# Banded attention with a feed-forward branch: score blocks in pairs on four PSUM banks shared with the attention outputs

## Chip, cores and metric

The kernel runs on one core of one Trainium2 chip, in one launch. The metric is the device time of that launch in microseconds (us); less is better. All inputs and outputs are float32.

## What is computed

x is 8 batches of 1024 rows of 512 numbers. Each row is normalised (mean, variance), and on the result stand an attention branch and a feed-forward branch, both added to x:

```python
def _L0_attn_ref(x, Wq, bq, Wk, bk, Wv, bv, Wo, bo):       # 16 heads of 64, N = 1024, E = 512
    Q = (x @ Wq + bq).reshape(B, N, 16, 64).transpose(0, 2, 1, 3)      # K and V in the same way
    scores = jnp.einsum('bhid,bhjd->bhij', Q, K)
    band = jnp.abs(idx[None, :] - idx[:, None]) <= 64
    columns = jnp.where(band, scores, 0.0)                 # outside the band the score is 0, not -inf
    attn = jax.nn.softmax(columns, axis=-1)
    out = (attn @ V).transpose(0, 2, 1, 3).reshape(B, N, 1024)
    return out @ Wo + bo

def _L0_ffn_ref(x, Win, bin_, W1, b1, W2, b2, Wout, bout):  # M = 64, INNER = 16
    s = x @ Win + bin_
    h = relu(s[..., None] * W1 + b1)
    g = einsum('btmh,mh->btm', h, W2) + b2
    return g @ Wout + bout

xn = layernorm(x)
return x + _L0_attn_ref(xn, ...) + _L0_ffn_ref(xn, ...)
```

## The kernel before

Five instruction streams (TensorE `pe`, VectorE `dve`, ScalarE `act`, GpSimd `pool`, SyncE `sp`) are written out by hand and meet at counting semaphores. There is no scheduler: the order in the code is the order on each engine. Each number that is multiplied is split into a high part and a low part of float32r, and each product is three passes (`PASSES`: high by high, high by low, low by high).

**Steps.** The work is a pipeline of 66 steps, one for each of 8 batches x 8 pairs of heads, and two to run out. Step n projects values, queries and keys of unit n (a pair of heads; `project`, line 811), attends for unit j = n - 1 (scores, softmax, weighting of the values), and projects out for unit o = n - 2 (`project_out`, line 822, eight tiles of 128 rows). `run_steps` writes out the steps: pairs 2 to 5 of a batch are an inner hardware loop (`middle`), batches 1 to 7 an outer one. Pairs 0 and 1 of a batch also carry the feed-forward branch (`ffn_first`, `ffn_last`), pair 6 the statistics of the next batch, pair 7 its normalisation (`ln_next`), pair 0 the last transposes of it (`ln`). 64 steps attend.

**Scores.** `scores(tp)`, for tp = 0 to 3, is two tiles of 128 queries, each against 256 keys, for both heads of the pair: 3 passes x 2 heads x 2 tiles = 12 matmuls. A head has 64 rows, so the two heads' matmuls stand in the two halves of the array and are recorded as a pair (x2). The results go to the two banks `score[0]` and `score[1]`, one for each head. VectorE's `mask_scores(tp)` (line 594) multiplies them by the band mask into `probs`, takes the row maxima and counts `masked`, four for each block. `scores(tp)` waits until the block before it is masked, since there is one pair of banks.

**Softmax and outputs.** ScalarE's `exps(tp)` (line 382) takes the exponentials, VectorE's `denominators(half)` (line 604) the reciprocals, GpSimd's `normalise_weights(half)` (line 301) scales. TensorE transposes the weights (`transpose_weights(u)`, line 867, into `pT_ps`) and weighs the values (`weigh_values(u)`, line 884) for u = 0 to 3, where u % 2 is the head and u // 2 the half of the queries; the result goes to bank `o_ps[h]`. ScalarE copies one half of it (`output_half(u)`, line 427), VectorE adds (`output_sum(u)`, line 647), counting `o_summed`, four for each step. `weigh_values(u)` waits for `o_summed` 4j + u - 1.

**The order around the change.** TensorE in a step: scores(0), V half 0, out(0), scores(1), out(1), V half 1, scores(2), out(2), Q half 0, scores(3), out(3), transposes of u = 0, out(4), and so on, to weigh_values(2), weigh_values(3), eight transposes of the values (line 856). V half 0 goes to bank `fill[0]` and waits for `v_lo` of the step before (line 653). out(0) goes to `fill[1]`, out(1) to `fill[0]`, which ScalarE's `value_lines(0)` (line 398) must have read (`v_in`). V half 1 goes to `fill[1]` and waits for the addition of out(0) on VectorE (`add_output`, line 615, `out_added`). out(4) waits for `qk_lo`, which VectorE counts when it has made `qT_lo` (`qk_low`, line 630) behind ScalarE's `qk_high` (line 412).

VectorE in a step: mask(0), out(0)'s addition, mask(1), out(1)'s addition, denominators(0), mask(2), out(2)'s addition, `qk_low(0)`, out(3)'s addition, mask(3), `weights_low(0)`; at the end out(7)'s addition, `qk_low(3)`, output_sum(2), values_low(0), output_sum(3), values_low(1). ScalarE at the end: output_half(2), values_high(0), output_half(3), values_high(1); values_high(0) waits for the transposes of the values.

The eight PSUM banks before are `fill` (2), `score` (2), `pT_ps` (2), `o_ps` (2).

Of the kernel before, what the change touches and what calls it, by code (L numbers as in the profile page):

```python
# [22 lines left out]
ACT = mybir.ActivationFunctionType  # L23
# [15 lines left out]
def band_attention_ffn(nc, x, Wq, bq, Wk, bk, Wv, bv, Wo, bo, Win, bin_, W1, b1, W2, b2, Wout, bout, out):  # L39
# [14 lines left out]
    with ExitStack() as ctx:  # L54
# [56 lines left out]
        fill = [bank("fill0"), bank("fill1")]  # L111
        score = [bank("score0"), bank("score1")]
        pT_ps = [bank("pT_ps0"), bank("pT_ps1")]
        o_ps = [bank("o_ps0"), bank("o_ps1")]
        ffn_banks = pT_ps + fill
# [228 lines left out]
        def _(act):  # L344
# [18 lines left out]
            for i in range(3):  # L363
# [3 lines left out]
            act.wait_ge(bias_T, 1)  # L367
            act.activation(bias_qkv[:].rearrange("p i h o -> p (i h o)"), score[0][:, 0:3 * PAIRS], ACT.Copy) \
                .then_inc(bias_in, 1)
# [3 lines left out]
            def step(n, b, pair, proj=True, attend=True, ln=False, ln_next=False, ffn_first=False, ffn_last=False,  # L373
# [49 lines left out]
                def output_half(u):  # L423

                    h = u % 2
                    act.wait_ge(pv_done, 4 * j + u + 1)
                    act.activation(o_part[h][h * D:h * D + D], o_ps[h][D - h * D:2 * D - h * D], ACT.Copy) \
                        .then_inc(o_half, 1)
# [118 lines left out]
        def _(dve):  # L547
# [33 lines left out]
            def step(n, b, pair, proj=True, attend=True, out_proj=True, ln=False, ln_next=False, stats_next=False,  # L581
# [4 lines left out]
                def mask_scores(tp):  # L586
                    due = in_register(dve, 4 * j + tp + 1)
                    dve.wait_ge(scored, 1)
                    dve.wait_ge(scored, due)
                    for h in range(2):  # L590
                        for i in range(2):
                            c, t = column(tp, h, i), 2 * tp + i

                            dve.tensor_tensor_reduce(out=probs[:, h, t], in0=score[h][:, i * WIN:i * WIN + WIN],  # L594
                                                     in1=mask[:], scale=1.0, scalar=0.0, op0=ALU.mult, op1=ALU.max,
                                                     accum_out=row_max[:, c:c + 1]).then_inc(masked, 1)
                    dve.wait_ge(masked, 16 * j + 4 * tp + 4)
                    cols = slice(4 * tp, 4 * tp + 4)
                    dve.tensor_scalar(neg_max[:, cols], row_max[:, cols], -1.0, None, ALU.mult).then_inc(max_ready, 1)  # L599
# [40 lines left out]
                def output_sum(u):  # L640
                    h, half = u % 2, u // 2
                    rows = slice(h * D, h * D + D)
                    dve.wait_ge(o_half, 4 * j + u + 1)
                    dve.wait_ge(v_back_ready, j + 1)
                    if h == 0 and begun(2 * j - 1 + half):
                        dve.wait_ge(oT_lo, 2 * j - 1 + half)
                    dve.scalar_tensor_tensor(o_sum[half][rows], o_ps[h][rows], v_back[rows], o_part[h][rows],
                                             ALU.add, ALU.add).then_inc(o_summed, 1)
# [134 lines left out]
        def _(pe):  # L783
# [3 lines left out]
            pe.wait_ge(const_in, 16 * N_CONST)  # L787
            pe.transpose(score[0][:, 0:3 * PAIRS], bias_rows[:], ident[0:3 * PAIRS, 0:3 * PAIRS]).then_inc(bias_T, 1)

            def step(n, b, pair, proj=True, attend=True, out_proj=True, ln=False, ln_next=False,  # L790
                     ffn_first=False, ffn_last=False, after_ffn=False, **_):
                j, o = n - 1, n - 2
                def scores(tp):
                    if tp == 0:
                        pe.wait_ge(qk_lo, 4 * j + 4)
                    if begun(16 * j + 4 * tp):
                        pe.wait_ge(masked, 16 * j + 4 * tp)
                    for i in range(2):
                        t = 2 * tp + i
                        for a, (qp, kp) in enumerate(PASSES):  # L800
                            for h in range(2):
                                rows = slice(h * D, h * D + D)
                                last = pe.matmul(score[h][:, i * WIN:i * WIN + WIN], qT[qp][rows, t * P:t * P + P],  # L803
                                                 kT[kp][rows, t * P:t * P + WIN], start=(a == 0), stop=(a == 2))
# [67 lines left out]
                def weigh_values(u):  # L872
                    half, h = u // 2, u % 2
                    pe.wait_ge(pT_lo, 8 * j + 2 * u + 2)
                    if u == 0:
                        pe.wait_ge(v_lo, 2 * j + 2)
                    if begun(4 * j + u - 1):
                        pe.wait_ge(o_summed, 4 * j + u - 1)
                    for k in range(5):
# [3 lines left out]
                        for part in (hi, lo):  # L883
                            last = pe.matmul(o_ps[h][:, q0:q0 + (end - first) * P],  # L884
                                             v[:, (4 * half + k) % T, h].rearrange("p a d -> p (a d)"),
# [8 lines left out]
                if attend:  # L894
                    scores(0)
                if ln:
                    transpose_x(b, 4)
                    transpose_x(b, 5)
# [15 lines left out]
                if ln:  # L914
                    transpose_x(b, 6)
                    transpose_x(b, 7)
                if attend:
                    scores(1)
                if out_proj and not proj:
# [12 lines left out]
                if attend:  # L932
                    scores(2)
                if out_proj and not proj:
                    project_out_last(2)
# [3 lines left out]
                if proj:  # L939
                    pe.wait_ge(v_in, 2 * n + 2)  # L940
                    project(Q_, 0, qk_proj, fill[QK_BANK[0]])
                if attend:
                    scores(3)
                if out_proj and not proj:
# [118 lines left out]
```

## Time and profile before

| | us |
|---|---|
| median of 3 runs | 2547.38 |
| lowest, highest | 2533.61, 2549.32 |
| span of the profiled execution | 2553.6 |
| TensorE busy in it | 2428.0 (95%) |
| VectorE busy | 1987.7 (78%) |
| ScalarE busy | 1701.5 (67%) |
| GpSimd busy | 1208.9 (47%) |

The rows in the section further down are all of the profiled execution. A row of the timeline has its start in us, its length in us, the engine, the line of the code, the operation, output <- inputs and a count; in brackets stands how long the engine was idle before it, and for whom it waited. Matmuls overlap: what counts is the distance from one start to the next. A row of the waits has who waited for whom, the total in us, how many times, and the longest. A row of the windows has the stretch, its length, then each engine's busy us with its count of instructions (TensorE's matmuls, its weight loads, VectorE, ScalarE, GpSimd), the clock that TensorE was granted (1.00 is all of it), the share of the DMA engines and GB/s.

### The profile page before, as it was taken

Reading aid. Unit: us, or ns where it says so; the run is one execution under the profiler, and the core shown is the slowest. Engines: PE = TensorE matmul, PEld = TensorE weight load, DVE = VectorE, ACT = ScalarE, POOL = GpSimd, SP = SyncE. Lnnn points to the kernel's source line nnn. Section 1 sums busy time; section 2 is a strip of 40 time slices with the busy share of each in tenths; the row PEclk is TensorE's granted clock in tenths of the full one; section 3 lists DMA queues with packets and bytes.
Section 4 is the critical chain, followed back from the end, with each engine's and each line's share of the span. In section 5 each row is a group of like instructions: output and inputs, shape, how many; then the busy total and the mean of one; then the engine's idle time right before and its main releaser. Section 6 shows DMA issues by size and latency. Waiting matters only on the chain.

```text
span 2553.6 us, 50140 instructions
## 1 busy us (share of the span) xinstructions
PE 2428.0 (95%) x14913; PEld 2006.8 (79%) x14913; DVE 1987.7 (78%) x5025; ACT 1701.5 (67%) x4458; POOL 1208.9 (47%) x1515
## 2 busy tenths in 40 slices
PE   4999999999999999999999999999999999999997
PEld 3788787888778787787877878778887788878886
DVE  3777888778887788777887777877779778797777
ACT  3666776667766677666775667756677666766665
POOL 2444445445454454544454444544546444464443
PEclk9999999999999999999999999999999999999999
DMA  3010112110121110201103011031010210012101
GB/s 118 22 30 20 34 30 87 33 34 18 34 83 33 34 29 23 92 24 34 34 17 100 21 30 34 17 100 33 18 34 19 98 33 30 22 52 65 33 21 38
DMA packets 130239, 106.04 MB, mean 42 GB/s; under 512 B 5736, under 2 KB 104064, under 8 KB 130048
## 3 DMA queue, kind: packets, MB, share of 16 engines
q1 hardware_dynamic: 130048, 103.72, 13.3%
q8 instruction: 92, 1.51, 0.3%
q14 instruction: 99, 0.81, 0.1%
HBM read 86.93 MB, written 16.78 MB: 41 GB/s over the span
## 4 chain that ended last, share of the span: by engine, by line
PE 71%; DVE 7%; issue 6%; ACT 6%; DMA 4%; POOL 3%; SPq 1%; DVEq 0%; ACTq 0%; POOLq 0%
PE fill L811 33%; PE fill L822 12%; PE o_ps L884 9%; PE pT_ps L867 7%; PE score L803 5%; ACT probs L382 3%; DMA w_raw<-in_L_attn_Wv 2%; DVE probs L594 2%; DMA out_x<-acc 2%; POOL acc L314 1%; POOL probs L301 1%; PE fill L856 1%; PE fill L849 1%; PE pT_ps L841 1%; ACT v L439 1%
## 5 line engine op out<-in xcount | busy, mean ns | idle before, releaser
L301 POOL TENSOR_SCALAR probs<-probs,inv_l,neg_e 128x256 f32<-128x256 f32 x1024 | 598.7, 598 | 778.6 <-DVE neg_e L609 778.6
L811 PE MATMUL fill<-xT_hi,w_hi 128*128 128x512 f32 x1536 | 627.0, 408 | 26.3 <-ACT vT L404 6.7
L382 ACT ACTIVATE probs<-probs,neg_max 128x256 f32<-128x256 f32 x1024 | 510.8, 501 | 154.1 <-DVE neg_max L599 152.4
L811 PE MATMUL fill<-xT_lo,w_hi 128*128 128x512 f32 x1536 | 608.5, 396 | 0.0
L811 PE MATMUL fill<-xT_hi,w_lo 128*128 128x512 f32 x1536 | 605.9, 394 | 0.0
L615 DVE TENSOR_TENSOR acc<-fill,acc 128x512 f32 (+1 forms) x512 | 350.6, 685 | 100.8 <-PE fill L822 93.6
L594 DVE CUSTOM_DVE_ANT_0 probs<-score,mask 128x256 f32<-128x256 f32 x1024 | 372.5, 421 | 33.6 <-issue 20.6
L811 PEld LDWEIGHTS fill<-xT_hi,w_hi 128*128 128x128 f32 x1536 | 293.7, 191 | 108.7 <-issue 26.6
L420 ACT ACTIVATE pT_hi<-pT_ps 128x512 fp32r<-128x512 f32 x512 | 278.2, 592 | 137.4 <-PE pT_ps L867 137.4
L307 POOL TENSOR_TENSOR oT_lo<-o_sum,oT_hi 128x512 fp32r<-128x512 f32 x128 | 171.1, 1337 | 411.3 <-ACT oT_hi L434 411.3
L811 PEld LDWEIGHTS fill<-xT_hi,w_lo 128*128 128x128 f32 x1536 | 292.5, 190 | 65.4
L811 PEld LDWEIGHTS fill<-xT_lo,w_hi 128*128 128x128 f32 x1536 | 293.6, 191 | 56.1
L637 DVE TENSOR_TENSOR pT_lo<-pT_ps,pT_hi 128x512 fp32r<-128x512 f32 x512 | 327.9, 682 | 1.4 <-ACT pT_hi L420 1.3
L884 PE MATMUL o_ps<-pT_hi,v 128*128 128x256 f32 (+1 forms) x1280 | 307.8, 279 | 0.0
L884 PE MATMUL o_ps<-pT_lo,v 128*128 128x256 f32 (+1 forms) x1280 | 305.5, 279 | 0.0
L867 PEld LDWEIGHTS pT_ps<-ident,probs 128*128 128x128 f32 x2048 | 242.8, 142 | 47.2 <-DVE pT_lo L637 9.8
L867 PE MATMUL pT_ps<-ident,probs 128*128 128x128 f32 x2048 | 273.5, 277 | 6.3 <-DVE pT_lo L637 4.8
L280 POOL TENSOR_TENSOR w_lo<-w_raw,w_hi 128x512 fp32r<-128x512 f32 x192 | 248.0, 1292 | 52.6 <-ACT w_hi L349 52.6
L822 PE MATMUL fill<-wo_hi,oT_hi 128*128 128x512 f32 x512 | 233.9, 457 | 32.1 <-DVE acc L615 21.6
L884 PEld LDWEIGHTS o_ps<-pT_lo,v 128*128 128x128 f32 x1280 | 243.2, 190 | 2.6
L884 PEld LDWEIGHTS o_ps<-pT_hi,v 128*128 128x128 f32 x1280 | 242.5, 189 | 2.6
L630 DVE SCALAR_TENSOR_TENSOR qT_lo<-fill,bias_qkv,qT_hi 128x512 fp32r<-128x512 f32 x128 | 95.8, 748 | 147.2 <-ACT qT_hi L412 147.2
(104 smaller groups left out, 4252.2 us busy)
## 6 DMA issues: line engine op xcount, KB each, us to landing
w_raw<-in_L_attn_Wv SPq DMA_DIRECT2D x64, 256.0 KB, 3.3
w_raw<-in_L_attn_Wq SPq DMA_DIRECT2D x64, 256.0 KB, 3.7
w_raw<-in_L_attn_Wk SPq DMA_DIRECT2D x64, 256.0 KB, 2.7
acc<-in_L_attn_x SPq DMA_DIRECT2D x8, 2048.0 KB, 9.3
wo_raw<-in_L_attn_Wo SPq DMA_DIRECT2D x64, 256.0 KB, 2.8
out_x<-acc SPq DMA_DIRECT2D x7, 2048.0 KB, 7.7
acc<-in_L_attn_x SPq DMA_DIRECT2D x2, 1024.0 KB, 6.7
out_x<-acc SPq DMA_DIRECT2D x2, 1024.0 KB, 4.3
```

Source lines behind the costliest of these rows:

```text
L280: pool.tensor_tensor(w[lo][:, i], w_raw[:, i], f32(w[hi][:, i]), ALU.subtract).then_inc(w_lo, 1)
L301: pool.tensor_scalar(probs[:, h, t], probs[:, h, t], inv_l[:, c:c + 1], neg_e[:, c:c + 1], ALU.mult, ALU.add).then_inc(normed, 1)
L307: pool.tensor_tensor(oT[lo][:, cols], o_sum[half][:], f32(oT[hi][:, cols]), ALU.subtract) \
L382: act.activation(probs[:, h, t], probs[:, h, t], ACT.Exp, bias=neg_max[:, c:c + 1], accum_out=row_sum[:, c:c + 1])
L420: act.activation(pT[u % 2][hi][:, k * LINE:k * LINE + LINE], pT_ps[k][:], ACT.Copy) \
L594: dve.tensor_tensor_reduce(out=probs[:, h, t], in0=score[h][:, i * WIN:i * WIN + WIN], in1=mask[:], scale=1.0, scalar=0.0, op0=ALU.mult, o ...
L615: dve.tensor_tensor(acc[:, parity, t], bank[:], acc[:, parity, t], ALU.add).then_inc(out_added, 1)
L637: dve.tensor_tensor(pT[u % 2][lo][:, cols], pT_ps[k][:], f32(pT[u % 2][hi][:, cols]), ALU.subtract).then_inc(pT_lo, 1)
L811: last = pe.matmul(dst[:], w[wp][:, i, k], xT[xp][:, k, half * LINE:half * LINE + LINE], start=(k == 0 and a == 0), stop=(k == KC - 1 and ...
L822: last = pe.matmul(dst[:], oT[op][:, t * P:t * P + P], wo[wp][:], start=(a == 0), stop=(a == 2))
L867: last = pe.transpose(pT_ps[k][:, i % 4 * P:i % 4 * P + P], probs[:, h, t, c * P:c * P + P], ident[:])
L884: last = pe.matmul(o_ps[h][:, q0:q0 + (end - first) * P], v[:, (4 * half + k) % T, h].rearrange("p a d -> p (a d)"), pT[h][part][:, first ...
```

## The change

The four banks of scores and outputs become one pool `attn[0..3]`. Block tp of the scores goes to `attn[2 * (tp % 2) + h]`, so blocks 0 and 2 have banks 0 and 1, blocks 1 and 3 banks 2 and 3. The output of u goes to `attn[u]`. On TensorE, scores(1) moves up to stand directly behind scores(0), and scores(3) directly behind scores(2). The waits follow the banks: scores(0) waits for the first two output sums of the step before, scores(1) for all four of them (`o_summed` 4j), scores(2) and scores(3) for the masks of two blocks before; `weigh_values(0)` and `weigh_values(2)` wait for the masks of blocks 2 and 3, and no longer for `o_summed`. The order of VectorE, ScalarE and GpSimd is as before, and no instruction is added or left out.

```diff
-        score = [bank("score0"), bank("score1")]
+        attn = [bank(f"attn{i}") for i in range(4)]
+        score = [[attn[2 * i + h] for h in range(2)] for i in range(2)]
+        o_ps = attn
         pT_ps = [bank("pT_ps0"), bank("pT_ps1")]
-        o_ps = [bank("o_ps0"), bank("o_ps1")]
...
                 def scores(tp):
                     if tp == 0:
                         pe.wait_ge(qk_lo, 4 * j + 4)
-                    if begun(16 * j + 4 * tp):
-                        pe.wait_ge(masked, 16 * j + 4 * tp)
+                    if tp >= 2:
+                        pe.wait_ge(masked, 16 * j + 4 * tp - 4)
+                    elif begun(4 * j + 2 * tp - 2):
+                        pe.wait_ge(o_summed, 4 * j + 2 * tp - 2)
...
-                                last = pe.matmul(score[h][:, i * WIN:i * WIN + WIN], qT[qp][rows, t * P:t * P + P],
+                                last = pe.matmul(score[tp % 2][h][:, i * WIN:i * WIN + WIN], qT[qp][rows, t * P:t * P + P],
...
                 def weigh_values(u):
-                    if begun(4 * j + u - 1):
-                        pe.wait_ge(o_summed, 4 * j + u - 1)
+                    if h == 0:
+                        pe.wait_ge(masked, 16 * j + 4 * half + 12)
...
-                            last = pe.matmul(o_ps[h][:, q0:q0 + (end - first) * P],
+                            last = pe.matmul(o_ps[u][:, q0:q0 + (end - first) * P],
...
                 if attend:
                     scores(0)
+                    scores(1)
                 if ln:
                     transpose_x(b, 4)
                     transpose_x(b, 5)
...
-                if attend:
-                    scores(1)
...
                 if attend:
                     scores(2)
+                    scores(3)
...
-                if attend:
-                    scores(3)
```

`output_half`, `output_sum` and `mask_scores` name the new banks (`o_ps[u]`, `score[tp % 2][h]`) and are otherwise the same.

On TensorE, in the inner loop, between out(0) and out(1) (the row of line 822 at the top is the last matmul of out(0), the one at the bottom the first of out(1); `score` is the block scores(1)), before:

```order
L822 MATMUL fill<-wo_hi,oT_lo 128x512
L797 REGISTER_ALU
L803 MATMUL score<-kT_hi,qT_hi 128x256 [waits masked]
L803 MATMUL score<-kT_hi,qT_hi 128x256
L803 MATMUL score<-kT_lo,qT_hi 128x256 x2
L803 MATMUL score<-kT_hi,qT_lo 128x256 x2
L803 MATMUL score<-kT_hi,qT_hi 128x256 x2
L803 MATMUL score<-kT_lo,qT_hi 128x256 x2
L803 MATMUL score<-kT_hi,qT_lo 128x256 x2
L922 REGISTER_ALU
L822 MATMUL fill<-wo_hi,oT_hi 128x512 [waits v_in]
```

The same place in the changed kernel, where line 825 is `project_out`:

```order
L825 MATMUL fill<-wo_hi,oT_hi 128x512 [waits oT_lo]
L825 MATMUL fill<-wo_lo,oT_hi 128x512
L825 MATMUL fill<-wo_hi,oT_lo 128x512
L924 REGISTER_ALU
L825 MATMUL fill<-wo_hi,oT_hi 128x512 [waits v_in]
```

Block 1 is gone from between them: out(1) with its wait for `v_in` stands directly behind out(0).

On TensorE, in the inner loop, at the start of a step of the changed kernel (`attn` is scores here; the first row is the last pair of scores(0), line 811 the wait ahead of V half 0 and line 814 its first matmul):

```order
L806 MATMUL attn<-kT_hi,qT_lo 128x256 x2
L806 MATMUL attn<-kT_hi,qT_hi 128x256 [waits o_summed]
L806 MATMUL attn<-kT_hi,qT_hi 128x256
L806 MATMUL attn<-kT_lo,qT_hi 128x256 x2
L806 MATMUL attn<-kT_hi,qT_lo 128x256 x2
L806 MATMUL attn<-kT_hi,qT_hi 128x256 x2
L806 MATMUL attn<-kT_lo,qT_hi 128x256 x2
L806 MATMUL attn<-kT_hi,qT_lo 128x256 x2
L907 ISA
L811 ISA [waits ffn_added,v_lo]
L814 MATMUL fill<-xT_hi,w_hi 128x512 [waits w_lo]
```

Before, the same place was this:

```order
L803 MATMUL score<-kT_hi,qT_lo 128x256 x2
L903 ISA
L808 ISA [waits ffn_added,v_lo]
L811 MATMUL fill<-xT_hi,w_hi 128x512 [waits w_lo]
```

Block 1 with its wait for `o_summed` now stands between scores(0) and V half 0.

## Rows read from the trace of the kernel before

**Rows 1.** The page: span, and busy us, share and instructions of each engine.
```profile
span 2553.6 us, 50140 instructions
PE 2428.0 (95%) x14913; PEld 2006.8 (79%) x14913; DVE 1987.7 (78%) x5025; ACT 1701.5 (67%) x4458; POOL 1208.9 (47%) x1515
```

**Rows 2.** The waits of TensorE: us in total, times, longest us.
```profile
PE score L803 <- issue: 15.3, 6, 2.7
PE fill L822 <- DVE qT_lo L630: 9.4, 7, 1.8
PE fill L811 <- ACT vT L404: 6.7, 9, 1.8
PE fill L811 <- DVE v L653: 5.1, 21, 0.2
PE score L803 <- DVE row_max L594: 4.6, 4, 2.0
```

**Rows 3.** The timeline of TensorE, step n = 3, from scores(0) to V half 1.
```profile
149.96 0.28 PE L803 MATMUL score<-kT_hi,qT_lo 64*128 64x256 f32 x2
150.38 0.49 PE L811 MATMUL fill<-xT_hi,w_hi 128*128 128x512 f32 x1
...
153.00 0.39 PE L811 MATMUL fill<-xT_hi,w_lo 128*128 128x512 f32 x1
...
153.68 0.39 PE L822 MATMUL fill<-wo_hi,oT_lo 128*128 128x512 f32 x1
154.00 0.39 PE L803 MATMUL score<-kT_hi,qT_hi 64*128 64x256 f32 x2
154.22 0.28 PE L803 MATMUL score<-kT_lo,qT_hi 64*128 64x256 f32 x2
...
154.69 0.28 PE L803 MATMUL score<-kT_hi,qT_lo 64*128 64x256 f32 x2
154.90 0.50 PE L822 MATMUL fill<-wo_hi,oT_hi 128*128 128x512 f32 x1
155.24 0.40 PE L822 MATMUL fill<-wo_lo,oT_hi 128*128 128x512 f32 x1
...
155.72 0.40 PE L811 MATMUL fill<-xT_hi,w_hi 128*128 128x512 f32 x1
```

**Rows 4.** The timeline of VectorE in the same step.
```profile
149.56 0.69 DVE L653 TENSOR_TENSOR v<-fill,v 128x512 fp32r<-128x512 f32 x1 [0.88 <-ACT v L439]
150.28 0.76 DVE L647 SCALAR_TENSOR_TENSOR o_sum<-o_ps,v_back,o_part 64x512 f32<-64x512 f32 x1
...
155.12 0.42 DVE L594 CUSTOM_DVE_ANT_0 probs<-score,mask 128x256 f32<-128x256 f32 x1
...
164.46 0.75 DVE L630 SCALAR_TENSOR_TENSOR qT_lo<-fill,bias_qkv,qT_hi 128x512 fp32r<-128x512 f32 x1 [2.38 <-ACT qT_hi L412]
165.12 0.68 DVE L615 TENSOR_TENSOR acc<-fill,acc 128x512 f32<-128x512 f32 x1
165.72 0.42 DVE L594 CUSTOM_DVE_ANT_0 probs<-score,mask 128x256 f32<-128x256 f32 x1
```

**Rows 5.** The timeline of ScalarE: the eviction of V half 0.
```profile
153.43 0.60 ACT L398 ACTIVATE vT<-fill 128x512 f32<-128x512 f32 x1 [1.11 <-PE fill L811]
153.92 0.19 ACT L398 ACTIVATION_READ_ACCUMULATOR vT<-fill 128x1 f32 x1
```

**Rows 6.** The timeline of TensorE: the first matmul of out(4).
```profile
165.63 0.48 PE L822 MATMUL fill<-wo_hi,oT_hi 128*128 128x512 f32 x1
```

**Rows 7.** Windows: step n = 3, and step n = 9, the second of a batch.
```profile
149.26:184.91 35.65, 35.50 (x225) 29.68 (x224) 27.45 (x73) 23.83 (x67) 16.74 (x22) 1.00 0.10 29
376.77:420.81 44.04, 42.44 (x251) 33.76 (x250) 40.95 (x90) 33.05 (x77) 28.69 (x29) 1.00 0.19 63
```

**Rows 8.** The timeline of TensorE, step n = 50: a matmul behind a wait of 1.78.
```profile
2001.08 0.49 PE L822 MATMUL fill<-wo_hi,oT_hi 128*128 128x512 f32 x1 [1.78 <-DVE qT_lo L630]
```

**Rows 9.** Windows: after that wait, and after one of 2.0 in the last step.
```profile
2003.00:2008.00 5.00, 5.00 (x32) 4.42 (x31) 4.50 (x11) 4.82 (x14) 1.84 (x4) 1.00 0.00 0
2516.00:2520.00 4.00, 3.77 (x27) 2.83 (x27) 2.99 (x12) 3.30 (x14) 0.00 (x0) 0.64 0.00 0
```

More of the change, by code:

```diff
@@ L367, in _ @@
             act.wait_ge(bias_T, 1)
-            act.activation(bias_qkv[:].rearrange("p i h o -> p (i h o)"), score[0][:, 0:3 * PAIRS], ACT.Copy) \
+            act.activation(bias_qkv[:].rearrange("p i h o -> p (i h o)"), attn[0][:, 0:3 * PAIRS], ACT.Copy) \
                 .then_inc(bias_in, 1)
@@ L426, in output_half @@
                     act.wait_ge(pv_done, 4 * j + u + 1)
-                    act.activation(o_part[h][h * D:h * D + D], o_ps[h][D - h * D:2 * D - h * D], ACT.Copy) \
+                    act.activation(o_part[h][h * D:h * D + D], o_ps[u][D - h * D:2 * D - h * D], ACT.Copy) \
                         .then_inc(o_half, 1)
@@ L592, in mask_scores @@
                             c, t = column(tp, h, i), 2 * tp + i
-                            dve.tensor_tensor_reduce(out=probs[:, h, t], in0=score[h][:, i * WIN:i * WIN + WIN],
+                            dve.tensor_tensor_reduce(out=probs[:, h, t], in0=score[tp % 2][h][:, i * WIN:i * WIN + WIN],
                                                      in1=mask[:], scale=1.0, scalar=0.0, op0=ALU.mult, op1=ALU.max,
@@ L646, in output_sum @@
                         dve.wait_ge(oT_lo, 2 * j - 1 + half)
-                    dve.scalar_tensor_tensor(o_sum[half][rows], o_ps[h][rows], v_back[rows], o_part[h][rows],
+                    dve.scalar_tensor_tensor(o_sum[half][rows], o_ps[u][rows], v_back[rows], o_part[h][rows],
                                              ALU.add, ALU.add).then_inc(o_summed, 1)
@@ L787, in _ @@
             pe.wait_ge(const_in, 16 * N_CONST)
-            pe.transpose(score[0][:, 0:3 * PAIRS], bias_rows[:], ident[0:3 * PAIRS, 0:3 * PAIRS]).then_inc(bias_T, 1)
+            pe.transpose(attn[0][:, 0:3 * PAIRS], bias_rows[:], ident[0:3 * PAIRS, 0:3 * PAIRS]).then_inc(bias_T, 1)
             def step(n, b, pair, proj=True, attend=True, out_proj=True, ln=False, ln_next=False,
```

## The prediction, made before the changed kernel was run

> **What bounds the kernel now.** I read the page first: its span and the busy shares [rows 1]. TensorE is busy for 95% of 2553.6 us, VectorE for 78%, so anything that makes TensorE wait or lets it run closer together moves the end one for one, unless another engine was about to be waited for. Next come TensorE's waits [rows 2]: apart from the lead-in and the eight steps around a batch's first pairs they are small, and no row there names an attention output or `o_summed`. Last, one ordinary step (the fourth, n=3) in order of time, on TensorE [rows 3], VectorE [rows 4] and ScalarE [rows 5]. What the reader is to see there: TensorE pays for each visit to the scores, and VectorE and ScalarE work through a chain that runs behind it with little room.
>
> I call the first value projection of a step V0, the second V1, the first query projection Q0, and the output projections out(0) to out(7).
>
> **The gain.** A score block is 12 matmuls on 64 rows, in pairs, between matmuls on all 128 rows. In [rows 3], around scores(1): the last full matmul starts at 153.68, the first score pair at 154.00, 0.32 later where full matmuls follow each other in 0.24 (155.24 to 155.72 is two of them): 0.08. The second pair comes 0.22 after the first, where pairs otherwise follow in 0.12 (154.22 to 154.69 is four of them): 0.10. Going out, 154.69 to 154.90 is 0.21 instead of 0.12: 0.09, and 154.90 to 155.24 is 0.34 instead of 0.24: 0.10. Together 0.37; with 0.23 as the pace, which V0 shows (153.00 to 153.68 is three matmuls), it is 0.39, and I take that. The change removes two such visits in each of 64 steps: 128 x 0.39 = 50 us. [...]
>
> **The new wait.** Score block 1 now writes banks 2 and 3 of the shared four, which the last two attention outputs of the previous step used. It waits for `o_summed` 4j, so for the previous step's last `output_sum`, and stands directly behind scores(0). In [rows 4] that addition runs from 150.28 to 151.04. A release of TensorE by VectorE takes 0.13: `v` ends at 150.25 and V0, which waits for it, starts at 150.38 [rows 3, 4]. So scores(1) starts at 151.17. It could have started at 149.96 + 0.12 = 150.08: a wait of 1.09 us. Queued behind it on TensorE is everything. Its six pairs take 0.22 + 4 x 0.12, then 0.21 to leave: V0 starts at 152.08 instead of 150.38, 1.70 later (of this, 0.70 is work that came earlier than before, and the 0.2 that V0 waited in any case is used up).
>
> Does it hit every step? Not the first step (nothing before it), not the eight that follow the feed-forward output (24 matmuls stand between), not the six that follow the end of the inner loop, where TensorE already sat up to 2.7 us with no named releaser [rows 2]. 64 - 1 - 8 - 6 = 49 steps have it.
>
> **What stood behind scores(1).** scores(1) used to lie between out(0) and out(1), and was cover. out(1) needs the eviction of V0's bank by ScalarE: that starts 0.43 after V0's last matmul (153.00 to 153.43) and its accumulator read ends 0.68 later [rows 5]; with 0.13 for the release, out(1) may start 1.24 after V0's last matmul. TensorE would be there after 4 x 0.23 = 0.92. So out(1) loses 0.32 and starts 153.00 + 1.70 + 1.24 = 155.94, which is 1.04 later than 154.90. V1 follows at 156.76; the first output addition, begun 0.43 after out(0)'s last matmul (155.38), takes 0.69 [rows 4] and is released at 156.63, so it does not stop V1. After V1 the second merge gives back its 0.39: +0.65 from there.
>
> **What is late next.** VectorE keeps its order, so mask(1) stands behind that addition: 155.81 + 0.60 (the pace from 165.12 to 165.72) = 156.41 where it was 155.12. The chain mask(1), exponentials, denominators, mask(2), exponentials, `qT_hi`, `qT_lo` passes back and forth between VectorE and ScalarE and moves as a whole by 1.29. `qT_lo` ends at 164.46 + 0.75 + 1.29 = 166.50 [rows 4], and Q0's own later end puts it some 0.07 further; TensorE is released at 166.7. out(4), which waits for it, would have started at 165.63 [rows 6] + 0.65 = 166.28. It loses 0.4. The step is then 1.05 us longer. VectorE catches up at the step's end, where it waits for out(7), so the next step starts from the same picture.
>
> **The sum.** In later batches V0 waited some 0.1 longer already (21 small waits, [rows 2]), so I take 1.0 for the 26 ordinary steps: 26 us. The eight steps that normalise the next batch have ScalarE later still: Q0 already waits for ScalarE there, one of the nine of [rows 2], so the whole 1.29 comes through: 8 x 1.3 = 10. In the seven steps with n = 9, 17, ... VectorE is busy for 40.95 of 44.04 us [rows 7], no room for a lag: 7 x 1.3 = 9. In the seven first steps of a batch (n = 8, 16, ...) the transposes of the new x also stand behind scores(1), and their evictions stand ahead of mask(0) on VectorE; I carry 1.8 of the 1.9 that TensorE is late: 7 x 1.8 = 13. The six behind the loop end: first merge free, but mask(0) and its additions were late there already, 0.15 each: 1. The eight after the feed-forward output: scores(1) is free, out(1) loses its cover, and in seven of them out(4) waits for `qT_lo` anyway, up to 1.8 [rows 2]: 0. First and last step: -1. Sum: 26 + 10 + 9 + 13 + 1 + 0 - 1 = +58. The profiled execution would go from 2553.6 to 2611.6. Its own time lies 6 above the median of the three runs, 2547.4, so I predict 2605 us.
>
> The other edits cost nothing: the outputs' wait for `masked` instead of `o_summed` is met microseconds before by mask(2) and mask(3), which the same engine's later work depends on; scores(2) and scores(3) wait for masks that are two blocks old. If that cover went, it would be at most one mask block, four times 0.42 us [rows 4].
>
> Bounds of the terms: the 1.09 wait is read to 0.05. What the lag adds is the soft part. If none of it reaches TensorE, the direct terms stand alone: 49 waits leave 0.65 each, less 0.1, and 15 free steps give back up to 0.78: 27 - 12 = +15. If the whole 1.9 of V0's delay and more contention came through in the 22 special steps and 1.29 in the ordinary ones, it is 26 x 1.3 + 22 x 1.9 = +76.
>
> **The rivals.**
> *Only direct terms* (+15, 2562 us; down to 0): ScalarE's exponentials catch up in their gaps. For it: VectorE sat idle 2.38 us before `qT_lo` [rows 4]. Against it: that gap is named as waiting for ScalarE, so it belongs to the chain.
> *The merge wins*, the other side of zero. Place: scores(1) at the step's start. Price: the `o_summed` wait. If that wait were below about 0.45 us instead of 1.09, out(1) and the chain would barely move and the 0.78 a step would win; with no wait at all, 2547 - 50 = 2497 us, with half the gain 2520. For it: the toll is plainly in [rows 3]. Against it: the last `output_sum` ends at 151.04 by its own chain, behind two evictions on ScalarE, which the change does not touch.
> [...]
>
> **How the numbers follow.** My forecast 0.72 (its own range 2580 to 2625), direct terms only 0.14, the merge wins 0.06, the clock 0.08. Range: 2562 to 2630 holds the forecast and most of the direct case, and leaves out the clock and the merge's win. A measurement of this kernel can tell about 1% from no change, that is 25 us. Faster by over 1%: 0.05. Within 1%: 0.15, the direct case and a part of the merge's. Slower by over 1%: 0.80.
>
> **What would show it.** TensorE's waits should hold a new row, `attn` scores behind `o_sum`, 49 times, mean 0.9 to 1.1, some 50 us in all; a row of out(1) behind `vT` (0.3 each); and out(4) behind `qT_lo` far above its 7 of now. The score blocks should come in pairs without the 0.22 and 0.34 in the middle. An ordinary step should take 36.7 instead of 35.65 [rows 7]. Wrong it would be if the last `output_sum` came earlier than 1.8 us after scores(0) begins, or if `qT_lo` were ready when out(4) comes.

## The result and the profile after

| | before | after |
|---|---|---|
| median of 4 runs | 2541.7 us | 2602.9 us |
| lowest, highest | 2533.6, 2549.3 | 2594.1, 2617.3 |
| span of the profiled execution | 2553.6 | 2592.4 |

The change makes the kernel slower: 1.025 times the time, interval 1.020 to 1.030. Run again (e11, below) it was 1.023, 1.021 to 1.026. The forecast was 2605 us and slower. It stood on a median of 2547.4 before; a fourth run brings that to 2541.7.

The page of the changed kernel, with its span, its engines and the chain of work that ended last, answers to [rows 1]:

```profile
span 2592.4 us, 49953 instructions
PE 2409.6 (93%) x14913; PEld 1997.7 (77%) x14913; DVE 1978.6 (76%) x5025; ACT 1693.5 (65%) x4458; POOL 1210.8 (47%) x1515
...
PE 54%; DVE 16%; ACT 15%; issue 11%; DMA 2%; POOL 1%; SPq 1%; DVEq 1%; ACTq 0%; POOLq 0%
```

TensorE is busy 18 us less, and the span is longer: it waits. The 18 us do not measure the gain of the merges: a step as below has 35.40 where it had 35.50 [rows 7], and with the guard of e6 on both sides the difference is 4 us (2414.9 in e6, 2410.5 in e9). The waits of TensorE and of its weight loads, changed kernel (engine, line, for whom: us in total, times, longest), where [rows 2] had nothing of the first, 7 of the second and nothing of the third:

```profile
PE attn L806 <- DVE o_sum L648: 56.4, 55, 2.7
PE fill L825 <- DVE qT_lo L631: 36.7, 53, 2.3
...
PEld fill L825 <- ACT vT L399: 28.6, 55, 0.5
```

The ordinary step n = 3 of the changed kernel, TensorE in order of time; line 806 is the scores, 814 the projections, 825 the output projection. It answers to [rows 3] and [rows 6]:

```profile
150.32 0.28 PE L806 MATMUL attn<-kT_hi,qT_lo 64*128 64x256 f32 x2
151.45 0.38 PE L806 MATMUL attn<-kT_hi,qT_hi 64*128 64x256 f32 x2 [0.86 <-DVE o_sum L648]
...
152.35 0.50 PE L814 MATMUL fill<-xT_hi,w_hi 128*128 128x512 f32 x1
...
155.02 0.39 PE L814 MATMUL fill<-xT_hi,w_lo 128*128 128x512 f32 x1
...
156.19 0.50 PE L825 MATMUL fill<-wo_hi,oT_hi 128*128 128x512 f32 x1
...
167.07 0.49 PE L825 MATMUL fill<-wo_hi,oT_hi 128*128 128x512 f32 x1 [0.37 <-DVE qT_lo L631]
```

The step begins at 149.62. scores(1) waits until the last output sum is there. V0 starts 2.73 us into the step where it was 1.12 (150.38 - 149.26), out(1) at 6.57 instead of 5.64, and out(4) at 17.45 instead of 16.37, behind `qT_lo`. VectorE and ScalarE in the same step, answering to [rows 4, 5]:

```profile
150.64 0.76 DVE L648 SCALAR_TENSOR_TENSOR o_sum<-attn,v_back,o_part 64x512 f32<-64x512 f32 x1
...
156.13 0.69 DVE L616 TENSOR_TENSOR acc<-fill,acc 128x512 f32<-128x512 f32 x1 [1.33 <-PE fill L825]
156.74 0.41 DVE L595 CUSTOM_DVE_ANT_0 probs<-attn,mask 128x256 f32<-128x256 f32 x1
...
166.19 0.75 DVE L631 SCALAR_TENSOR_TENSOR qT_lo<-fill,bias_qkv,qT_hi 128x512 fp32r<-128x512 f32 x1 [2.54 <-ACT qT_hi L413]
```

```profile
155.45 0.60 ACT L399 ACTIVATE vT<-fill 128x512 f32<-128x512 f32 x1 [2.78 <-PE fill L814]
155.94 0.19 ACT L399 ACTIVATION_READ_ACCUMULATOR vT<-fill 128x1 f32 x1
...
165.34 0.69 ACT L413 ACTIVATE qT_hi<-fill,bias_qkv 128x512 fp32r<-128x512 f32 x1
```

The last output sum ends 1.78 us into the step, as before (151.04 - 149.26). mask(1) starts at 7.12 instead of 5.86: VectorE now waits 1.33 for out(0).

Windows of the changed kernel (stretch, length, busy us of TensorE, its weight loads, VectorE, ScalarE, GpSimd, clock, DMA share, GB/s): step 3, then 16 and 17 (the first two of a batch), then 10 and 18 (the third of a batch), which answer to [rows 7]:

```profile
149.62:186.35 36.73, 35.40 (x225) 29.66 (x224) 27.32 (x73) 23.74 (x67) 16.69 (x22) 1.00 0.10 29
654.31:699.27 44.96, 41.73 (x257) 34.42 (x257) 35.86 (x82) 31.98 (x78) 23.18 (x26) 1.00 0.07 21
699.27:744.15 44.88, 42.26 (x250) 33.89 (x250) 41.13 (x91) 32.57 (x77) 28.41 (x29) 1.00 0.19 59
425.84:465.11 39.27, 37.14 (x227) 30.66 (x226) 26.36 (x71) 21.13 (x62) 13.70 (x20) 0.96 0.29 96
744.15:781.59 37.44, 35.16 (x227) 29.61 (x226) 25.36 (x71) 20.90 (x62) 14.14 (x20) 1.00 0.30 100
```

One row does not fit. Step 16 took 46.87 in the first profile of the kernel before:

```profile
642.66:689.53 46.87, 43.80 (x257) 36.47 (x257) 37.18 (x82) 31.89 (x78) 22.60 (x26) 0.93 0.07 20
```

So here the changed kernel is faster by 1.9 us, where the forecast had it 1.8 slower, and the two profiles differ by only 39 us where the medians differ by 61. Experiments e5, e6, e9 and e11 are about that.

### The profile page after: what moved, and what is told of

Its sections match the earlier page's. It is cut to its first block, busy times and chain, and to the rows that moved or that the text cites. A ratio compares the mean times of both kernels' runs of the same rounds, so it can differ in the third digit from the quotient of the medians.

```text
span 2592.4 us, 49953 instructions
## 1 busy us (share of the span) xinstructions
PE 2409.6 (93%) x14913; PEld 1997.7 (77%) x14913; DVE 1978.6 (76%) x5025; ACT 1693.5 (65%) x4458; POOL 1210.8 (47%) x1515
## 4 chain that ended last, share of the span: by engine, by line
PE 54%; DVE 16%; ACT 15%; issue 11%; DMA 2%; POOL 1%; SPq 1%; DVEq 1%; ACTq 0%; POOLq 0%
PE fill L814 25%; PE attn L887 9%; ACT probs L383 8%; PE fill L825 8%; PE pT_ps L870 5%; DVE probs L595 5%; PE attn L806 3%; DVE o_sum L648 2%; DVE qT_lo L631 2%; ACT qT_hi L413 2%; ACT v L440 1%; DVE acc L616 1%; PE fill L852 1%; PE fill L859 1%; PE pT_ps L844 1%
## 5 line engine op out<-in xcount | busy, mean ns | idle before, releaser
L595 DVE CUSTOM_DVE_ANT_0 probs<-attn,mask 128x256 f32<-128x256 f32 x1024 | 371.8, 419 | 23.6 <-PE attn L806 14.0
L887 PE MATMUL attn<-pT_hi,v 128*128 128x256 f32 (+1 forms) x1280 | 307.8, 279 | 0.0
L887 PE MATMUL attn<-pT_lo,v 128*128 128x256 f32 (+1 forms) x1280 | 305.5, 279 | 0.0
L870 PEld LDWEIGHTS pT_ps<-ident,probs 128*128 128x128 f32 x2048 | 237.4, 140 | 55.8 <-DVE pT_lo L638 15.2
L825 PE MATMUL fill<-wo_hi,oT_hi 128*128 128x512 f32 x512 | 225.6, 441 | 47.5 <-DVE qT_lo L631 36.7
L887 PEld LDWEIGHTS attn<-pT_lo,v 128*128 128x128 f32 x1280 | 243.2, 190 | 2.6
L887 PEld LDWEIGHTS attn<-pT_hi,v 128*128 128x128 f32 x1280 | 242.5, 189 | 2.6
L806 PE MATMUL attn<-kT_hi,qT_hi 64*128 64x256 f32 x1024 | 164.6, 317 | 57.2 <-DVE o_sum L648 56.4
```

The costliest lines, as they stand in the source:

```text
L595: dve.tensor_tensor_reduce(out=probs[:, h, t], in0=score[tp % 2][h][:, i * WIN:i * WIN + WIN], in1=mask[:], scale=1.0, scalar=0.0, op0=ALU ...
L806: last = pe.matmul(score[tp % 2][h][:, i * WIN:i * WIN + WIN], qT[qp][rows, t * P:t * P + P], kT[kp][rows, t * P:t * P + WIN], start=(a == ...
L825: last = pe.matmul(dst[:], oT[op][:, t * P:t * P + P], wo[wp][:], start=(a == 0), stop=(a == 2))
L870: last = pe.transpose(pT_ps[k][:, i % 4 * P:i % 4 * P + P], probs[:, h, t, c * P:c * P + P], ident[:])
L887: last = pe.matmul(o_ps[u][:, q0:q0 + (end - first) * P], v[:, (4 * half + k) % T, h].rearrange("p a d -> p (a d)"), pT[h][part][:, first ...
```

## The experiments

Each ratio is against runs of the kernel before on the same chip, and is one of means, with its 95% interval; the times are medians. "Step" is the ordinary step n = 4 of a profile; it takes 35.65 before and 36.74 after.

| | what | us | against before | step |
|---|---|---|---|---|
| e1 | only blocks 2, 3 together | 2550.9 | 1.003 (0.998 to 1.008) | 35.81 |
| e2 | only blocks 0, 1 together | 2596.3 | 1.021 (1.015 to 1.027) | 36.59 |
| e3 | changed, last output first | 2544.2 | 1.001 (0.996 to 1.006) | 35.61 |
| e4 | before, one more visit to the scores | 2571.9 | 1.011 (1.004 to 1.017) | 36.01 |
| e6 | before, with a guard | 2524.9 | 0.990 (0.988 to 0.992) | 35.65 |
| e7 | e3, blocks 0, 1 only, guard | 2521.5 | 0.989 (0.987 to 0.990) | 35.50 |
| e8 | before, with the wait alone | 2583.7 | 1.013 (1.011 to 1.015) | 36.52 |
| e9 | changed, with the guard | 2586.6 | 1.021 (1.019 to 1.022) | 36.73 |
| e10 | e7, first two steps of a batch as before | 2515.9 | 0.992 (0.991 to 0.994) | 35.50 |
| e11 | changed, once more | 2593.7 | 1.023 (1.021 to 1.026) | 36.73 |

The kernel before had medians of 2535.8 (beside e1 to e4), 2551.2 (e5 to e8) and 2534.5 (e9 to e11).

### Is there a toll for each visit to the scores? (e4)

scores(3) of the kernel before is cut in two, one tile on either side of out(3):

```diff
-                    scores(3)
+                    scores(3, (0,))
                 ...
                     project_out(3)
+                if attend:
+                    scores(3, (1,))
```

> The kernel before with one more visit to the scores in each step: the two tiles of block 3 stand apart, the second behind out(3). Nothing else moves, and mask(3) comes 0.9 us after it. If a visit costs a toll of 0.39 us: 64 x 0.39 = +25 us, 2567 us, and an ordinary step of 36.0. If the toll is a matter of the block's first matmuls being weighed wrongly in the records: no change.

It came to 2571.9 us, 1.011, and the step to 36.01: 0.36 longer. The toll stands at the size that was read from single rows. TensorE in e4, step 4, shows it in the last three pairs ahead of out(3): 0.23 from the first to the second, and 0.34 from out(3)'s first matmul to its second. Behind out(3) the next visit begins in the same way (202.19, then 202.41), and it ends at the transposes. In e4's profile the ordinary steps are 0.34 longer than before on average; those behind the feed-forward output, the second ones of a batch and those that normalise are 0.15 to 0.32 longer.

```profile
200.73 0.38 PE L803 MATMUL score<-kT_hi,qT_hi 64*128 64x256 f32 x2
200.96 0.28 PE L803 MATMUL score<-kT_lo,qT_hi 64*128 64x256 f32 x2
201.07 0.28 PE L803 MATMUL score<-kT_hi,qT_lo 64*128 64x256 f32 x2
201.28 0.50 PE L823 MATMUL fill<-wo_hi,oT_hi 128*128 128x512 f32 x1
201.62 0.40 PE L823 MATMUL fill<-wo_lo,oT_hi 128*128 128x512 f32 x1
```

### What does the wait cost alone? (e8)

```diff
                     if begun(2 * n - 1):
                         pe.wait_ge(v_lo, 2 * n - 1)
+                    if attend and begun(4 * j):
+                        pe.wait_ge(o_summed, 4 * j)
```

> The kernel before, order and banks unchanged, with one wait more: V0 waits for all output sums of the step before, as scores(1) does in the changed kernel. V0 then starts at 151.17 instead of 150.38 in the step shown: 0.79 later. My theory: VectorE and ScalarE go along with it, nothing else is lost since scores(1) still covers out(1): an ordinary step of 36.45, 49 x 0.75 = +37 us. If the lag of the chain itself costs more than TensorE's own delay, it would be 36.7 and above; if the steps have room, under 36.0.

It came to 2583.7 us, 32 more than before on that chip, and the step to 36.52, 0.87 longer than before. In order of time in e8 (step 4 begins at 186.20) V0 starts 1.98 in, 0.86 later than before. In this step its wait is laid to `v`, which was done 0.99 in; the output sum ended 1.78 in, and in 36 other steps the wait is laid to that:

```profile
186.90 0.28 PE L803 MATMUL score<-kT_hi,qT_lo 64*128 64x256 f32 x2
188.18 0.49 PE L811 MATMUL fill<-xT_hi,w_hi 128*128 128x512 f32 x1 [1.00 <-DVE v L653]
```

```profile
PE fill L811 <- DVE o_sum L647: 39.6, 36, 1.2
```

In an ordinary step the delay of V0 goes through to the step's length one for one (0.86 later, 0.87 longer); the first two steps of a batch and those that normalise are only 0.3 to 0.45 us longer than before on average. The wait alone, with order and banks as before, makes more than half of the loss. With the wait and both merges the step is 36.73, so two visits saved and one cover lost come out at worse than nothing.

### Which merge does what? (e1, e2)

e1 puts scores(1) back between out(0) and out(1); e2 puts scores(3) back behind Q0.

```diff
                     scores(0)
-                    scores(1)
...
+                    scores(1)
...
                     scores(2)
-                    scores(3)
...
+                    scores(3)
```

> The changed kernel with scores(1) back in its old place between out(0) and out(1); only blocks 2 and 3 stay together. My theory (the loss is the wait of scores(1) for the last output sum, and what stood behind it): that wait is over long before, the cover of out(1) is back, VectorE and ScalarE are not late. What is left is the gain of one merge, 0.39 us, of which out(4)'s wait for qT_lo may take 0.1: 64 x 0.3 = -19 us against before, 2523 us, and an ordinary step of 35.35. Rival (sharing the four banks, or the pairing itself, costs something): slower than before, 2560 or more.

> The changed kernel with scores(3) back in its old place; only blocks 0 and 1 stay together. My theory: in the changed kernel TensorE then waits 0.4 us at out(4) for qT_lo, so whatever the second merge saves is waited away there. Without it the ordinary step stays 36.7 us and the whole within 5 us of the changed kernel, 2600 to 2608. Rival (the tolls simply add): 64 x 0.39 = 25 us slower than the changed kernel, 2628, an ordinary step of 37.1.

e2 came nearly as expected: 2596.3, a step of 36.59, 0.15 shorter than the changed kernel's. The second merge saves nothing there. In e2's step 4 (it begins at 187.06) `qT_lo`, with Q0 in its old place, is 1.20 later than before, from VectorE's and ScalarE's chain alone. It ends 17.15 in, and out(4) starts at 17.28, without a wait:

```profile
203.46 0.75 DVE L631 SCALAR_TENSOR_TENSOR qT_lo<-fill,bias_qkv,qT_hi 128x512 fp32r<-128x512 f32 x1 [2.37 <-ACT qT_hi L413]
```

```profile
204.34 0.49 PE L825 MATMUL fill<-wo_hi,oT_hi 128*128 128x512 f32 x1
```

e1 was a miss: no gain, and a step 0.16 longer than before, though scores(1) is back in its place. Its waits name the reason:

```profile
PE fill L825 <- DVE qT_lo L631: 30.2, 44, 2.3
```

So does e1's step 4 (it begins at 186.19) on TensorE, VectorE and ScalarE. out(4) starts 16.53 in, not 16.37, behind `qT_lo`, which starts at 15.64 instead of 15.20:

```profile
202.72 0.49 PE L825 MATMUL fill<-wo_hi,oT_hi 128*128 128x512 f32 x1 [0.37 <-DVE qT_lo L631]
```

```profile
201.83 0.75 DVE L631 SCALAR_TENSOR_TENSOR qT_lo<-fill,bias_qkv,qT_hi 128x512 fp32r<-128x512 f32 x1 [2.87 <-ACT qT_hi L413]
```

```profile
200.98 0.69 ACT L413 ACTIVATE qT_hi<-fill,bias_qkv 128x512 fp32r<-128x512 f32 x1 [0.39 <-PE fill L814]
```

In e1 VectorE's and ScalarE's chain is not late at all. But scores(3) now stands ahead of Q0, Q0 ends later by its 0.7 us, ScalarE waits 0.39 for it, and `qT_hi`, `qT_lo` and out(4) follow. The transposes ahead of out(4) begin 0.47 earlier than before (15.12 in, not 15.59), and out(4) 0.16 later: the merge saves, and more than that is waited away. In the eight steps that normalise the next batch the second merge does pay: they are 0.17 shorter in e1 than before, and 0.12 shorter in the changed kernel than in e2. That was in reach of the trace before: in [rows 4] `qT_lo` ends at 165.21 and out(4) starts at 165.63 [rows 6], 0.4 later. Any move of work ahead of Q0 by more than that becomes a wait.

### Is it the wait for the last output sum? (e3)

ScalarE and VectorE take the last output ahead of the values; banks and TensorE's order are those of the changed kernel.

```diff
-                if proj:
-                    values_high(0)
                 if attend:
                     output_half(3)
+                if proj:
+                    values_high(0)
...
-                if proj:
-                    values_low(0)
                 if attend:
                     output_sum(3)
+                if proj:
+                    values_low(0)
```

> The changed kernel, but at the end of a step ScalarE and VectorE take the last output (output_half(3), output_sum(3)) ahead of the first half of the values. My theory: the last output sum then ends about 0.95 us earlier, TensorE's wait ahead of scores(1) falls from 0.9 idle to 0.2 or less, V0 is 0.7 to 0.8 later than before (the work of block 1), out(1) still loses its cover, 0.3, and the second merge gives 0.39: an ordinary step of 35.4, and 10 to 25 us under before: 2527 us. Rival (the loss comes from pairing or banks, not from the wait): it stays above 2580.

The wait is gone. TensorE in e3, step 4 (it begins at 187.14): scores(1) begins at 187.96, 0.12 behind the last pair of scores(0), and V0 1.62 in.

```profile
187.84 0.28 PE L806 MATMUL attn<-kT_hi,qT_lo 64*128 64x256 f32 x2
187.96 0.28 PE L806 MATMUL attn<-kT_hi,qT_hi 64*128 64x256 f32 x2
...
188.76 0.50 PE L814 MATMUL fill<-xT_hi,w_hi 128*128 128x512 f32 x1
```

The step falls from 36.74 to 35.61 and the whole by some 2% against the changed kernel: the loss was that wait and what it drags behind it, neither the banks nor the pairing. But it is 1.001 of before, not the 10 to 25 us under it that I expected: the step is 0.04 shorter, not 0.25, since out(4) still waits for `qT_lo`, as e3's waits say:

```profile
PE fill L825 <- DVE qT_lo L631: 33.5, 53, 1.9
```

`qT_lo` starts 15.42 into the step, where it was 15.20 before. With Q0 back in its old place (e7, below) it is 15.34, so most of the 0.22 is the chain behind the lost cover, and 0.08 is the moved Q0.

### The first step of a batch (e5, e6, e9, e11)

In the first profile VectorE's subtraction from vT, which takes 0.75 or 0.86 us elsewhere (1.53 in the very first step), took 4.0 in the seven first steps of batches 2 to 8, and in each of them an output projection waited 3.1 us for an addition that VectorE does behind it. This row of TensorE's waits before is of those seven steps:

```profile
PE fill L822 <- DVE acc L615: 21.6, 7, 3.1
```

VectorE and GpSimd of the kernel before, step 16:

```profile
673.85 4.02 DVE L731 TENSOR_SCALAR vT<-vT,v_new 128x1024 f32<-128x1024 f32 x1
```

```profile
673.59 2.50 POOL L314 TENSOR_TENSOR acc<-acc,bias_row 128x512 f32 x2
676.06 1.26 POOL L280 TENSOR_TENSOR w_lo<-w_raw,w_hi 128x512 fp32r<-128x512 f32 x1
```

The changed kernel, step 16:

```profile
687.15 1.57 DVE L732 TENSOR_SCALAR vT<-vT,v_new 128x1024 f32<-128x1024 f32 x1
```

```profile
686.89 2.96 POOL L315 TENSOR_TENSOR acc<-acc,bias_row 128x512 f32 x2
```

Both times it runs beside GpSimd's additions on whole tiles of SBUF; it loses 3.2 or 0.7 us. Both lengths have one form: the subtraction ends 0.55 us after an instruction of GpSimd, at 4.02 after the third behind its start (677.32 to 677.87; the three take their usual 1.27 each), at 1.57 after the first (688.17 to 688.72), and then the next addition takes 1.72 instead of 1.27. From these ends I take it that the subtraction waits for a gap between two instructions of GpSimd and can miss two; no run shows what it waits for. e5 is the kernel before once more, with no edit.

> The kernel before once more, for a second profile. In the first one the seven first steps of a batch took 45.7 to 47.1 us, with VectorE's subtraction from vT at 4.0 us instead of 0.86; in the profile of e1, where that part of the step is the same, four of seven took 43.1. If this part differs from execution to execution, it is between 43.0 and 47 here too and not the same seven numbers; if it is fixed, the seven numbers repeat. An ordinary step stays 35.65 or 35.76 in both cases.

It took 2548.7 us, and the seven steps 45.6, 46.4, 46.0, 47.0, 43.3, 46.4, 45.9. Two of them in e5:

```profile
1266.06:1313.02 46.96, 43.89 (x257) 36.57 (x256) 37.18 (x82) 31.79 (x78) 22.63 (x26) 0.93 0.07 20
1578.93:1622.20 43.27, 41.85 (x258) 34.33 (x258) 35.56 (x82) 31.96 (x78) 23.23 (x26) 1.00 0.08 23
```

The subtraction took 4.0 in six of them and 1.57 in the step of 43.3. It is the same program, so the length differs from step to step; GpSimd's addition begins 0.26 ahead of it either way. In e6 GpSimd waits:

```diff
+                if ffn_first:
+                    pool.wait_ge(v_centered, n + 1)
                 if ffn_first or ffn_last:
                     add_biases([0, 1] if ffn_first else [4, 5])
```

> The kernel before, with GpSimd's additions of the bias (two tiles, in the first step of a batch) held until VectorE's subtraction from vT is done. If the two slow each other where they meet: the subtraction takes 0.9 us in all seven steps, the wait of 3.1 us ahead of an output projection and the slow clock behind it go, these steps take 43.0 us each time, and the whole is 5 to 15 us faster than before where the meeting was bad. Rival (the subtraction is slow for another reason): it stays at 4.0 in part of them and the time does not change.

The subtraction takes 0.75 us, GpSimd gives up 1.3, and all seven steps take 42.5. e6, on VectorE, on GpSimd, and the window of step 16:

```profile
667.71 0.75 DVE L733 TENSOR_SCALAR vT<-vT,v_new 128x1024 f32<-128x1024 f32 x1
```

```profile
668.80 2.53 POOL L314 TENSOR_TENSOR acc<-acc,bias_row 128x512 f32 x2 [1.31 <-DVE vT L733]
```

```profile
636.57:679.05 42.48, 41.63 (x257) 34.28 (x257) 34.79 (x82) 31.82 (x78) 22.90 (x26) 1.00 0.07 22
```

The wait for VectorE's addition ahead of the output projection is gone with it. The four runs of e6 lie within 2.3 us, 1.0% under before: more than I expected, since the slow clock behind the long wait went too (0.93 in the 46.96 above, 1.00 here). The 1.0% is against the kernel before on this chip, at 2551.2; on the two other chips it ran at 2535.8 and 2534.5, and there the kernel before was not run with the guard.

> The changed kernel with the guard of e6, so that the meeting of VectorE's subtraction and GpSimd's additions is out of both sides of the comparison. Against e6 (2525 us) my sum of +58 should then stand undisturbed: the seven first steps of a batch take 44.3 against 42.5 there (+1.8 each), an ordinary step 36.7 against 35.7, and the whole 2583 us. Rival (the seven first steps lost nothing by themselves, as the first pair of profiles read): 42.5 to 43.0 in these steps, and 2570.

> The changed kernel once more, on one chip with e9. In its first profile the subtraction from vT took 1.57 us in all seven steps and these took 45.0. If that is a matter of the moment, some are at 4.0 here and these steps at 46 to 49; if the changed kernel's timing has moved the two apart, it is 1.57 in all seven again. The guard then is worth 7 x 0.7 = 5 us here, not the 26 of the kernel before: 2588 where e9 is 2583.

e9 came to 2586.6, e11 to 2593.7, with 1.56 or 1.57 in all seven steps of e11, as in the first profile of the changed kernel. The guard is worth 7 us to the changed kernel and 26 to the one before, each on its own chip. In e9 step 16 takes 44.19, 1.7 more than in e6:

```profile
184.71:221.44 36.73, 35.40 (x225) 29.65 (x224) 27.41 (x73) 23.72 (x67) 16.67 (x22) 1.00 0.10 29
651.68:695.87 44.19, 41.55 (x257) 34.35 (x256) 35.07 (x82) 31.83 (x78) 22.80 (x26) 1.00 0.07 21
```

### Towards a faster kernel (e7, e10)

e7 is e3 with scores(3) behind Q0 again and the guard. e10 is e7 with scores(1) back ahead of out(1) in the first two steps of a batch:

```diff
+                early = not (ln or ffn_last)
                 if attend:
                     scores(0)
-                    scores(1)
+                    if early:
+                        scores(1)
...
+                if attend and not early:
+                    scores(1)
```

> e3 with scores(3) back in its old place, and the guard of e6. In e3 TensorE waits at out(4) until 16.3 us of a step for qT_lo, since Q0 stands behind scores(3). With scores(3) behind Q0 again, qT_lo is ready at about 16.1, so an ordinary step goes from 35.6 to 35.5, 0.25 under before; 49 to 60 steps of it are 12 to 15 us, with the guard 15 to 25 us under before. If the second merge were a gain in itself, this would be slower than e3: 36.0 a step.

> e7, but in the first two steps of each batch (7 each) scores(1) stands in its old place. In e7 these took 43.2 and 44.5 against 42.5 and 43.8 in e6, and the other steps were 0.2 to 0.3 shorter. If the loss there is scores(1) standing ahead of the transposes and of VectorE's long queue, both gains add: 42.5 and 43.8 again, 14 x 0.7 = 10 us under e7, about 1.5% under before (2511 where before is 2551). If it is the swapped order at the end of the step ahead of them, nothing changes against e7.

e7 came to 2521.5, on one chip with e6's 2524.9: 3 us under it and 30 under before, where 15 to 25 were expected. Its step is the expected 35.50, and by the profiles the 26 ordinary steps together are 8 us shorter than in e6, but the first two steps of a batch lost 0.8 and 0.6 each, 10 us in all. In e10 the first of these went back to 42.5, the second only from 44.49 to 44.41 where e6 has 43.84: half a miss. For the first the place of scores(1) was the cause. For the second the order at the end of the step ahead is left, as the rival had it, but no run has that order alone, so this is not shown. e10 is 0.992 (0.991 to 0.994) of before on a chip where before had 2534.5, e7 0.989 on one where it had 2551.2, so these two ratios do not rank them; their profiles, one each, have spans of 2512.9 and 2518.7, and 5.4 of the 5.8 us between them lie in the seven first steps. Both beat the kernel before and the changed one. Most of that is the guard, not the merge.

## Why the prediction was right, and where it was not

The sum by kinds of step, in us, of the forecast and of two pairs of profiles: after less before, and the same with the guard on both sides (e9 less e6, which ran on different chips; their ordinary steps are those of the first pair, 36.73 and 35.65).

| kind of step | forecast | after - before | e9 - e6 |
|---|---|---|---|
| 26 ordinary | +26 | +25.0 | +23.3 |
| 8 that normalise the next batch | +10 | +7.8 | +8.1 |
| 7 second ones (n = 9, 17, ...) | +9 | +5.8 | +7.2 |
| 7 first ones (n = 8, 16, ...) | +13 | -9.2 | +12.1 |
| 6 behind the loop's end | +1 | +1.5 | +2.3 |
| 8 behind the feed-forward output | 0 | +9.8 | +9.3 |
| first, last, ends | -1 | -1.8 | -1.1 |
| sum | +58 | +38.8 | +61.2 |

The sum of +58 against +61.2 is closer than its terms: one kind of step was put 9 us too low, and the ordinary, the normalising, the second and the first ones together 7 us too high. That the time came within 2 us of 2605 is in part luck, since single runs of the changed kernel spread over 23 us.

**The gain** of 0.39 for each visit held nearly: e4 has 0.36.

**The new wait** held in place and nearly in size. V0 was forecast 2.82 us into the step and came at 2.73. The release of scores(1) took 0.05 (151.40 to 151.45), not 0.13; here the matmul itself waits, where V0's wait stands in an instruction of its own. Whether that is the reason was not tried. The wait counts 55 times instead of 49, because the six steps behind the loop's end have it too: TensorE stood there in any case, now until the output sum. Of the 56.4 us, the 15.3 in six waits of [rows 2] are therefore not new.

**The lost cover** held: out(1) was forecast at 155.94 - 149.26 = 6.68 and came at 6.57, and its weight loads wait for `vT` 55 times.

**What is late next** held in size and in half of its reason. out(4) was forecast at 166.7 - 149.26 = 17.44 and came at 17.45. I laid it to the chain of VectorE and ScalarE, 1.29 late, and gave Q0's own lateness 0.07. The chain alone makes `qT_lo` 1.20 late (e2), and Q0 adds 0.17 (1.37 in the changed kernel). But the moved Q0 is also a cause by itself, which I had missed: with scores(1) back (e1) the chain is on time and out(4) waits all the same, for Q0. So this step of the prediction was wrong: "After V1 the second merge gives back its 0.39". In the ordinary steps it never paid, whatever the first merge does (e1: +0.16, e2 against the changed kernel: 0.15 better without it).

**The first steps of a batch**: +13 was right against a kernel in which the subtraction and GpSimd's additions do not meet (e9 - e6: +12.1). Against the first profile of before it reads -9.2, since that execution had the long form of it in all seven. A sum made against one execution inherits its accidents.

**The eight behind the feed-forward output** were put at 0 and cost 9 to 10: this is the term that was most mis-sized. That out(4) waits for `qT_lo` there in any case did not make the changes free. The wait, up to 1.8 before, is 1.9 to 2.3 in seven of the eight now. In four of them (steps 10, 26, 42 and 58, waits 2.00, 2.34, 2.00 and 2.03) the granted clock was 0.57 to 0.59 in the 4 us behind it, and the steps took 39.2 to 39.6; in the other three (18, 34 and 50, waits 2.18, 2.01 and 1.93) it was 1.00, and they took 37.2 to 37.4, about 2 us less. With the second merge alone (e1) the eight cost 5.8 us against before, with the first alone (e2) 3.2. The windows 2 us behind this wait in step 10 and 4 us behind it in step 18, changed kernel:

```profile
446.00:450.00 4.00, 4.00 (x21) 3.35 (x19) 2.28 (x7) 2.85 (x11) 1.14 (x3) 0.76 0.00 0
766.00:770.00 4.00, 4.00 (x28) 3.60 (x27) 3.51 (x9) 3.18 (x8) 2.65 (x5) 1.00 0.00 0
```

That is the fall of the clock to which the forecast gave 0.08, as behind the wait of 2.0 of [rows 9] and not behind the 1.78 of [rows 8]: in four of these eight steps, with waits of 2.00 to 2.34. The 49 waits of scores(1), forecast at 1.1, came at 0.70 to 0.86 and had none behind them, and the mean clock of the whole is 0.993 after, 0.987 before.

**The rivals.** Only the direct terms: no, e8 shows that in the ordinary steps the delay goes through whole. The merge wins: e3 fulfils its condition, no wait ahead of scores(1), and it still does not win, because the lost cover and the moved Q0 take it back.

## What to carry to other kernels

Work that is moved forward in an in-order stream is taken away as cover where it stood and put as delay ahead of everything behind its new place; look at both for the nearest wait with little slack (here 0.4 us between `qT_lo` and out(4)) before a gain per instruction is multiplied by its count. Buffers that are shared with a later stage bring that stage's last reader into the wait (here 0.86 us in an ordinary step): if they must be shared, let that reader go first on its engines (e3: the step fell from 36.74 to 35.61). And take two profiles of the kernel before: a stage whose length differs between identical steps was worth more here than the change at hand (26 us for the guard in e6, 3 more for the merge in e7).

## What was not expected of the hardware

VectorE's tensor_scalar on 128x1024 float32 in SBUF took 0.75 us alone, 1.57 or 4.02 us when GpSimd's tensor_tensor ran beside it, in the same program and even the same execution (e5), and holding GpSimd back by 1.3 us made the kernel 1.0% faster (e6). Wherever it took more than 0.75, it ended 0.54 to 0.56 after an instruction of GpSimd, in every profile. It lengthens GpSimd too: the addition beside the 1.57 took 1.72 instead of 1.27. No run shows why the two lengthen each other, or what decides between 1.57 and 4.02. A wait of TensorE of 2.00 us was followed by a granted clock of 0.59 in the next 4 us (step 10 of the changed kernel), one of 1.88 by 0.61 (e11, step 58), one of 2.18 by 1.00 (step 18), and the 49 waits of 0.70 to 0.86 of the changed kernel were each followed by 1.00.
